# Later layer norms of a perceiver kernel: mean on ScalarE, deviation folded into the transposing product

## The reference

```python
def _layernorm(x, axis=-1, eps=1e-05):
    m = jnp.mean(x, axis=axis, keepdims=True)
    v = jnp.var(x, axis=axis, keepdims=True)
    return (x - m) / jnp.sqrt(v + eps)

x = x + _L0_xattn_ref(_layernorm(x, axis=-1), ctx_2048)           # stage 0: 16 groups of channels
x = x + _L0_attn_ref(_layernorm(x, axis=-1), ...)                 # stage 1: 16 heads, rotary, causal
x = x + _L0_ffn_ref(_layernorm(x, axis=-1), ...)                  # stage 2: 32 experts and a shared one
x = x + _L1_xattn_ref(_layernorm(x, axis=-1), ctx_2048, mask)     # stage 3: one head over 4096 rows
x = x + _L1_attn_ref(_layernorm(x, axis=-1), ...)                 # stage 4: 32 heads, 8 for keys, rotary
x = x + _L1_ffn_ref(_layernorm(x, axis=-1), ...)                  # stage 5: 8 experts and a shared one
```

## Time and profile before

| | |
|---|---|
| median of 3 runs | 1435.17 us (1434.88 to 1435.29) |
| profiled execution, its own time | 1436.34 us |
| its span in the trace | 1434.6 us |
| TensorE busy | 1375.6 us (96%) |
| VectorE busy | 1151.8 us (80%) |
| ScalarE busy | 940.2 us (66%) |
| starts of stages 1 to 5 (first statistics) | 685.2, 756.5, 1062.9, 1176.9, 1301.7 us |

### The profile page before, as it was taken

The page is one execution under the profiler, slowest core; times in us unless marked ns, Lnnn a source line. Parts: engine busy times, 40 slices in busy tenths (PEclk is TensorE's granted clock), DMA queues, the critical chain, the costliest instruction groups (busy, mean ns, idle before and its releaser), DMA issues. The chain is left out here.

```text
span 1434.6 us, 27306 instructions
## 1 busy us (share of the span) xinstructions
PE 1375.6 (96%) x10680; PEld 837.0 (58%) x10680; DVE 1151.8 (80%) x1670; ACT 940.2 (66%) x1764; POOL 138.4 (10%) x171
## 2 busy tenths in 40 slices
PE   3999999999999999999899899999989889999998
PEld 2433333333333333333458899999978664567997
DVE  5999999999999999997486666666658456887665
ACT  1588888888888888888184545555434540785453
POOL 4122221221122222110000000000000000000000
PEclk9999999999999999999999999999999999999999
DMA  7544665555454455544205555544446514203651
GB/s 179 145 106 105 161 137 119 141 146 125 110 118 114 96 124 111 95 69 68 88 1 219 207 183 195 193 176 175 176 157 269 235 66 169 67 2 111 183 187 38
DMA packets 63281, 192.54 MB, mean 134 GB/s; under 512 B 32840, under 2 KB 33264, under 8 KB 51248
## 3 DMA queue, kind: packets, MB, share of 16 engines
q1 hardware_dynamic: 62976, 190.80, 46.4%
q10 hardware_dynamic: 192, 0.20, 0.1%
HBM read 165.72 MB, written 21.83 MB: 131 GB/s over the span
## 5 line engine op out<-in xcount | busy, mean ns | idle before, releaser
L530 DVE TENSOR_REDUCE pm<-bank 128x1 f32<-128x1024 f32 x512 | 621.3, 1221 | 14.9 <-PE bank L611 9.3
L589 ACT ACTIVATE probs<-bank 128x512 f32<-128x512 f32 x1024 | 554.5, 598 | 97.7 <-PE bank L630 92.2
L611 PE MATMUL bank<-kst,qst 48*128 48x512 f32 x1024 | 371.1, 452 | 21.9 <-DMA qst<-qsplit 20.1
L630 PE MATMUL bank<-qst,kst 52*128 52x512 f32 (+1 forms) x1024 | 372.4, 448 | 1.5 <-DVE pm L530 0.8
L647 PE MATMUL bank<-probs,vext 128*32 128x256 f32 x3968 | 316.7, 391 | 0.0
L630 PEld LDWEIGHTS bank<-qst,kst 52*128 52x128 f32 (+1 forms) x1024 | 153.0, 185 | 210.9 <-ACT probs L589 182.0
L1373 PE MATMUL bank<-e_xhi,e_hi 128*128 128x256 f32 (+1 forms) x768 | 219.4, 286 | 4.5 <-DVE e_lo L1308 3.9
L1373 PE MATMUL bank<-e_xlo,e_hi 128*128 128x256 f32 (+1 forms) x768 | 219.0, 285 | 0.0
L1373 PE MATMUL bank<-e_xhi,e_lo 128*128 128x256 f32 (+1 forms) x768 | 219.0, 285 | 0.0
L647 PEld LDWEIGHTS bank<-probs,vext 128*32 128x32 f32 x3968 | 78.1, 108 | 181.2 <-ACT probs L589 91.3
L611 PEld LDWEIGHTS bank<-kst,qst 48*128 48x128 f32 x1024 | 149.8, 186 | 29.4 <-DMA qst<-qsplit 20.1
(11 more groups left out here) (220 smaller groups left out, 1516.5 us busy)
## 6 DMA issues: line engine op xcount, KB each, us to landing
raw<-wall SPq DMA_DIRECT2D x43, 1536.0 KB, 6.5
kst<-kscratch SPq DMA_DIRECT2D x192, 128.0 KB, 4.5
kscratch<-ksplit SPq DMA_DIRECT2D x15, 1024.0 KB, 4.7
kraw<-ctx_rows SPq DMA_DIRECT2D x16, 512.0 KB, 6.3
vraw<-ctx_vt SPq DMA_DIRECT2D x16, 512.0 KB, 7.1
ctxT<-ctxT SPq DMA_DIRECT2D x8, 1024.0 KB, 11.9
nat<-ctx_chunks SPq DMA_DIRECT2D x6, 1024.0 KB, 22.1
weights<-wscratch SPq DMA_DIRECT2D x16, 256.0 KB, 3.5
```

Source lines behind the costliest of these rows:

```text
L530: nc.vector.tensor_reduce(pm[:, h % 2, r % 4, c:c + 1], bank[:, 2 * (r % 2):2 * (r % 2) + 2, :], AX.XY, ALU.max).then_inc(pre_reduced, 1)
L589: nc.scalar.activation(probs[:, (XST * k + n) % PR, :], bank[:, S_BANK[k][n], :], ACT.Exp, scale=XSCALE).then_inc(probs_ready, 1)
L611: ins = nc.tensor.matmul(bank[:, 2 * (r % 2) + j, :], qst[64 * j:64 * j + KR, h, tt * P:tt * P + P], kst[64 * j:64 * j + KR, h % 2, c * 51 ...
L630: nc.tensor.matmul(bank[:, S_BANK[k][n], :], kst[64 * j:64 * j + rows, h % 2, m * P:m * P + P], qst[64 * j:64 * j + rows, h, :], start=Tru ...
```

## The change

Stage 0 keeps its norm, under the name `first_norm_dve`. In stages 1 to 5 the normalized half is no longer written by VectorE. ScalarE takes the square root with epsilon as its bias, directly from `mv`, and then writes `xn = X - mean`, two 128x512 instructions with the negated mean (`minus`) as bias. VectorE writes `scaling`, the identity with each row multiplied by the token's inverse deviation, 128x128 for each half. TensorE turns and scales each block in one ordinary product, `xn` block transposed times `scaling`. TensorE waits for both, ScalarE's half and VectorE's matrix. The semaphore counts follow.

```diff
 def norm_dve(g, dve, k, link):
...
     for a in range(TA):
         ins = nc.vector.bn_aggr(g.mv[:, a, :], g.stats[:, a, :])
-    link(ins)
-    nc.vector.tensor_scalar(g.var[:, :, :], g.mv[:, :, 1:2], EPS, None, ALU.add).then_inc(g.var_ready, 1)
-    dve.wait_ge(g.std_ready, k + 1)
+    ins.then_inc(g.var_ready, 1)
+    dve.wait_ge(g.var_ready, 2 * k)
+    nc.vector.tensor_scalar(g.minus[:, :, :], g.mv[:, :, 0:1], -1.0, None, ALU.mult).then_inc(g.var_ready, 1)
+    link(nc.vector.tensor_scalar(g.var[:, :, :], g.mv[:, :, 1:2], EPS, None, ALU.add))
+    dve.wait_ge(g.std_ready, 3 * k - 1)
     link(nc.vector.reciprocal(g.rstd[:, :, :], g.std[:, :, :]))
...
     for a in range(TA):
-        nc.vector.tensor_scalar(g.xn[:, a, :], g.X[:, a, :], g.mv[:, a, 0:1], g.rstd[:, a, :],
-                                ALU.subtract, ALU.mult).then_inc(g.xn_ready, 1)
+        nc.vector.tensor_scalar(g.scaling[:, a, :], g.ident[:, :], g.rstd[:, a, :], None, ALU.mult).then_inc(g.xn_ready, 1)

 def norm_act(g, act, k):
...
-    act.wait_ge(g.var_ready, k + 1)
-    g.nc.scalar.activation(g.std[:, :, :], g.var[:, :, :], ACT.Sqrt).then_inc(g.std_ready, 1)
+    act.wait_ge(g.var_ready, 2 * k)
+    g.nc.scalar.activation(g.std[:, :, :], g.mv[:, :, 1:2], ACT.Sqrt, bias=g.eps[:, :]).then_inc(g.std_ready, 1)
+    act.wait_ge(g.var_ready, 2 * k + 1)
+    for a in range(TA):
+        g.nc.scalar.activation(g.xn[:, a, :], g.X[:, a, :], ACT.Identity, bias=g.minus[:, a, :]).then_inc(g.std_ready, 1)

 def norm_turn_pe(g, pe, k):
     keep_busy(g, 8, 5)
     for a in range(TA):
         pe.wait_ge(g.xn_ready, TA * k + a + 1)
+        pe.wait_ge(g.std_ready, 3 * k + a)
         for d in range(DC):
-            ins = g.nc.tensor.transpose(g.bank[:, 6 + a, d * P:d * P + P], g.xn[:, a, d * P:d * P + P], g.ident[:, :])
+            ins = g.nc.tensor.matmul(g.bank[:, 6 + a, d * P:d * P + P], g.xn[:, a, d * P:d * P + P], g.scaling[:, a, :],
+                                     start=True, stop=True)
         ins.then_inc(g.xn_turned, 1)
     keep_busy(g, 5, 5)
...
+            nc.gpsimd.memset(g.eps[:, :], EPS)
             nc.gpsimd.memset(ident[:, :], 0.0).then_inc(g.ident_ready, 1)
```

More of the change, by code:

```diff
@@ L136, in setup @@
     g.warm = sb("warm", [P, 1])
+    g.eps = sb("eps", [P, 1])
+    g.minus = sb("minus_mean", [P, TA, 1])
+    g.scaling = sb("scaling", [P, TA, P])
     g.arena_size = 184 * 1024
@@ L150, in setup, with first_norm_dve @@
     return g
-def norm_dve(g, dve, k, link):
+def first_norm_dve(g, dve, k, link):
     nc = g.nc
@@ L164, in norm_dve @@
     link(nc.vector.reciprocal(g.rstd[:, :, :], g.std[:, :, :]))
-    if k == 0:
-        for a in range(TA):
-            ins = nc.vector.tensor_scalar(g.std[:, a, :], g.rstd[:, a, :], g.rstd[:, a, :], None, ALU.mult)
-        link(ins)
[L170 to L181, removed]
+    for a in range(TA):
+        ins = nc.vector.tensor_scalar(g.std[:, a, :], g.rstd[:, a, :], g.rstd[:, a, :], None, ALU.mult)
+    link(ins)
+    for a in range(TA):
+        ins = nc.vector.tensor_scalar(g.std[:, a, :], g.std[:, a, :], -0.5, g.var[:, a, :], ALU.mult, ALU.mult)
+    link(ins)
+    for a in range(TA):
+        ins = nc.vector.tensor_scalar(g.rstd[:, a, :], g.std[:, a, :], 1.5, g.rstd[:, a, :], ALU.add, ALU.mult)
+    link(ins)
     for a in range(TA):
@@ L184, in norm_dve @@
                                 ALU.subtract, ALU.mult).then_inc(g.xn_ready, 1)
+def norm_dve(g, dve, k, link):
+    nc = g.nc
+    for a in range(TA):
+        ins = nc.vector.bn_stats(g.stats[:, a, :], g.X[:, a, :])
+    link(ins)
+    for a in range(TA):
+        ins = nc.vector.bn_aggr(g.mv[:, a, :], g.stats[:, a, :])
+    ins.then_inc(g.var_ready, 1)
[3 more added lines that the diff above has]
+    dve.wait_ge(g.std_ready, 3 * k - 1)
+    link(nc.vector.reciprocal(g.rstd[:, :, :], g.std[:, :, :]))
+    link(nc.vector.tensor_tensor(g.std[:, :, :], g.rstd[:, :, :], g.rstd[:, :, :], ALU.mult))
+    link(nc.vector.scalar_tensor_tensor(out=g.std[:, :, :], in0=g.std[:, :, :], scalar=-0.5, in1=g.var[:, :, :],
+                                        op0=ALU.mult, op1=ALU.mult))
+    link(nc.vector.scalar_tensor_tensor(out=g.rstd[:, :, :], in0=g.std[:, :, :], scalar=1.5, in1=g.rstd[:, :, :],
+                                        op0=ALU.add, op1=ALU.mult))
+    for a in range(TA):
+        nc.vector.tensor_scalar(g.scaling[:, a, :], g.ident[:, :], g.rstd[:, a, :], None, ALU.mult).then_inc(g.xn_ready, 1)
 def norm_act(g, act, k):
@@ L510, in _ @@
             dve.wait_ge(x_loaded, 16)
-            norm_dve(g, dve, 0, link)
+            first_norm_dve(g, dve, 0, link)
             for a in range(TA):
```

## The result

The changed kernel takes 1439.43 us (median of 10 runs, 1436.9 to 1442.39), the kernel before 1435.23 us (median of 10 runs, 1433.93 to 1437.82). The ratio of the two is 1.0028, 95% interval 1.0018 to 1.0038: slower by 4.0 us, clear of no change. The forecast was +3.0 us and 1438.2 us, in a range of 1436.1 to 1439.4 us. The change by the ratio, put on the 1435.17 us that the forecast started from, gives 1439.2 us; the median itself lies at the range's upper edge.

A forecast was written before the change was run, and what follows sets the result against it. TensorE, busy 96% of the span, was taken as the bound, with no step of a norm's chain hidden. Losses of 0.73 + 3 x 0.40 + 1.05 = 2.98 us took 1435.17 to 1438.2 us; range 1436.1 to 1439.4 us.

The forecast's parts named there:

- The turn: TensorE's eight block products per norm: sixteen passes of 0.113 us, 1.97 us against 1.11, a loss of 0.86 us.
- Rival D: In the turn, a pass costs weights and columns one after the other: 3.4 us a turn, 1444 us; chance 0.05.
- rival E: Not slower: eight products take the transpositions' 1.11 us, -0.2 us in all; chance 0.05.
- The reciprocal's 0.15 us: In each changed norm the reciprocal starts 0.31 us after `mv` instead of 0.46; gain 0.15 us (0.05 to 0.20).
- The last VectorE step: Writing `scaling` (287 ns) instead of half of `xn` (0.56 us) brings TensorE's operand 0.27 us earlier.
- Stages 2, 4 and 5: Turn starts 0.4 us earlier, lasts 0.86 longer; after the copies each stage loses 0.40 us (0.25 to 0.6).
- Stage 1: Unread products at half clock hide the earlier operand: gain 0.08, loss 0.86, less 0.05 for copies; 0.73 us lost.
- Stage 3: Two subtractions delay ScalarE's rounding, and through it TensorE, by 1.05 us (0.9 to 1.3); the longer turn is hidden.
- The sum: Losses of stages 1 to 5 together: 0.73 + 3 x 0.40 + 1.05 = 2.98 us.
- case A: Whole kernel: the summed losses with the clock's pattern as before, 1438.2 us (bounds +2.1 to +3.9); chance 0.50.
- rival B: The last stage's half-clock stretch, worth 1.7 us, is gone: +1.3 us, 1436.5 us; chance 0.30.
- factor of four: Four times a transposition's 0.12 us: a turn of 3.9 us, a norm losing 2.8; its chance within 0.05.

The follow-up runs named there:

- e3: The kernel before with each transposition of the five norms issued twice, sixteen one-pass instructions for eight; 1439.29 us, ratio 1.0030.
- e1: The changed kernel with each turn's eight products put back to transpositions and the scaling left out; 1438.97 us, ratio 1.0019.
- e5: The changed kernel with the root taken from `var` without a bias pointer, `minus` computed after `var`; one execution, 1441.46 us.
- e9: The changed kernel with twelve unread multiplications ahead of the turn in stages 2 to 5, six more behind stage 3's turn; 1439.72 us, ratio 1.0035.
- e2: The changed kernel with ScalarE, in stage 3 alone, rounding the first chunk ahead of the two subtractions; one profiled execution, 1438.56 us.
- e12: The kernel before with sixteen unread multiplications where TensorE waits for an expert's weights in stage 2; 1434.68 us, ratio 0.9998.
- e4: The kernel before with each unread multiplication around the five turns replaced by two unread transpositions; 1435.35 us, ratio 1.0001.

## Why the prediction was right, and where it was not

*The turn.* Right in kind and nearly in size: sixteen passes, 2.05 us against 1.97 forecast and 1.11 before. The pass took 0.118 us ((2.05 - 0.28) / 15) where I had taken 0.113. That is the step of the eight transpositions (0.119), but the sixteen of e3 have a step of 0.113, so what the 0.08 us are is open. e1 and e3 show the cost of the second passes from both sides. Rival D (weights and columns in turn) and rival E (one pass) are out.

*The reciprocal's 0.15 us.* Mis-sized: 0.04. The root starts 0.21 us sooner after `mv`, but takes 295 ns where it took 203, and the reciprocal follows its end by 0.10 us where it was 0.03. The two VectorE steps that now stand before the reciprocal aren't this delay: VectorE idles 0.16 us behind them, and e5, which has two as well, shows 0.03 again. The range I gave began at 0.05, too high by a hair.

*The last VectorE step.* `scaling` 283 ns, as taken from the row of L990 (287). With the reciprocal, TensorE's start moved from 1.86 to 1.56 us after `mv`: 0.30, not 0.4.

*Stages 2, 4 and 5.* 0.60, 0.64 and 0.60 us instead of 0.40 each, by the two terms above: 0.10 at the start and 0.08 in the turn. The rest, 0.02 to 0.06, is what I had let the copies take back: the second copy ends 0.62 us after the turn where it was 0.65, so they take back 0.03 and not 0.06. That stage 5's rounding would add nothing was right, though it starts 1.13 us later and not 0.9; in e1, whose turn is shorter, it does hold up the first copy.

*Stage 1.* 0.64 instead of 0.73. The step that the unread multiplications hide the earlier operand failed here: the clock rose earlier in their course, and the turn started at 688.01, 1.56 us after `mv` as in the other stages. In other executions the step does hold: in stage 1 of e9's profile the turn starts 1.80 us after `mv`.

*Stage 3.* 1.12 instead of 1.05; the subtractions are 713 ns, 1.33 us for both, near the upper row (718). The queue order is confirmed by e2: with the rounding first, 0.62 of the 1.12 us came back.

*The sum.* 0.64 + 0.60 + 1.12 + 0.64 + 0.60 = 3.60 us instead of 2.98; at full clock the runs differ by 3.5. The case A, the likeliest, is what came in kind. Its terms were 0.62 us too small together, and stage 2's late statistics (0.36 us) are in no term; the measured +4.0 us is just above the bounds that the terms gave (+2.1 to +3.9). That the result is at the range's edge and not beyond it is partly luck.

*The clock, rival B.* The one profile speaks for it: the stretch of the last stage was gone. The runs don't: 5.9 ± 0.7 us lost after, 5.6 ± 0.4 before. The stretch of the last stage is back in the profiles of e2 and e9, two kernels with the changed turn, and missing in that of e12, whose last stage is that of before. I had read a stretch of one execution as a property of the kernel. Chance 0.30 for its vanishing, and 0.08 for a new one, were both priced as if they came once and for all; they come and go from run to run. They make a good part of the 4 to 6 us by which the runs of one kernel mostly differ: over the 10 runs of after, and over the 20 of before beside e1, time and loss to the clock are correlated at 0.9. The chances of slower (0.43) and same (0.55) leaned on B; the change was slower.

The Trainium skill's sentence on four passes of true FP32 (FP8 and Floating Point Precision, TensorE Precision Notes) was weighed as a factor of four on the turn. The trace shows two records for a product, 2.05 us for a turn and 1.8 times the transpositions; by the factor of four it would have been 3.9 us. I had set the factor on the wrong thing. Against a bf16 product of 512 columns it does come out: the unread ones, eight in 1.89 us and a single one 0.38, have a step of (1.89 - 0.38) / 7 = 0.22 us, and a plain float32 product takes 2 x 0.43 = 0.86. A float32 transposition of 128 columns has a step of 0.12 us and the product of that size 0.24, a factor of two. The Trainium skill's sentence that transposition mode doesn't count as TensorE being busy in the same way (TensorE: Matmul & The Clock Gate, Part 4) doesn't fit e4, and the measurement decides: for float32 blocks of 128x128 the clock rose under transpositions alone, and the runs lost the same 5.6 us to it as with multiplications.

## What to carry to other kernels

Folding a scale into a transposition makes a plain float32 product of it, and this costs a second pass: on a path where nothing hides TensorE, eight blocks of 128x128 lost 0.94 us, while shortening VectorE's last step from 512 to 128 columns gave 0.26. Work moved to another engine must be read in that engine's queue: what stands behind it (here a rounding that releases VectorE and then TensorE) is delayed by all of it, even if the moved work itself is in time. Where the clock differs from run to run, compare distances between two events in the trace, and span times granted clock over many runs, not two spans. And look outside the changed stretch too: here 0.36 us came ahead of it, at the start of a stage.

## What the runs showed of the hardware that was not expected

A 128x2 root on ScalarE lasted 295 ns with a bias pointer, reading `mv`, and 203 without, reading `var`; no run separates the pointer from the operand. Cutting a 128x512 operation of VectorE (544 ns) into two of 128x256 gave 409 ns each, and four of these 1.38 us against 1.00 for two whole ones. The half-clock stretches came in or behind waits of 3 to 4 us, but also behind one of 1.95 us with 1.3 us of work since (stage 3 of the changed kernel, 1128 to 1131.5 us), and not behind the same wait in the kernel before. In the last stage of before, TensorE's longest wait was 1.54 us, four microseconds earlier. In the profiles they lasted 3.4 us or twice that.
